# A product of values and weights on VectorE whose inner dimension becomes the head

## The reference

```python
key_e = k[src] + e
alpha = jnp.sum(q[dst] * key_e, axis=-1) / jnp.sqrt(jnp.asarray(C, x.dtype))
m = jax.ops.segment_max(alpha, dst, num_segments=N)
p = jnp.exp(alpha - m[dst])
denom = jax.ops.segment_sum(p, dst, num_segments=N)
w = p / (denom[dst] + 1e-16)
msg = (v[src] + e) * w[..., None]
agg = jax.ops.segment_sum(msg.reshape(E, heads * C), dst, num_segments=N).reshape(N, heads, C)
```

## Time and profile before

| | |
|---|---|
| median of 3 runs | 7181.92 us (7181.11 to 7182.72) |
| profiled execution | 7166.77 us, its span 7165.0 us |
| busy over the span | PE 81%, POOL 67%, VectorE (DVE) 64%, ACT 47% |
| multi-head stage | about 2426 to 4846 us of the span |
| messages (L886) | 488 instructions, 332.3 us, 681 ns each |

### The profile page before, as it was taken

How to read it: one execution, slowest core, us unless ns; L and a number is a source line. 1 busy time by engine, 2 the same in 40 slices (tenths; PEclk the granted TensorE clock), 3 DMA queues, 4 the chain that set the end, 5 groups by cost and what they waited for, 6 DMA issues and landing times. The chain is left out here.

```text
span 7165.0 us, 172653 instructions
## 1 busy us (share of the span) xinstructions
PE 5823.4 (81%) x39803; PEld 4591.0 (64%) x39803; DVE 4571.8 (64%) x12911; ACT 3369.3 (47%) x8069; POOL 4776.0 (67%) x4738
## 2 busy tenths in 40 slices
PE   3688888898766577777777877876889999999997
PEld 2667777777764366666677767773555555666666
DVE  4344455555567577888889999995444555555554
ACT  2334444445444345555556666652334444444442
POOL 0677777777772377777777777642777777777760
PEclk7787888899887676777778787777999999999999
DMA  2455565566544666666666666656455555555552
GB/s 79 126 142 146 150 155 156 157 167 170 126 92 112 203 186 185 187 191 192 196 195 199 199 199 197 193 147 172 107 109 112 115 119 119 121 123 122 122 118 62
DMA packets 1111078, 1069.51 MB, mean 149 GB/s; under 512 B 399272, under 2 KB 882780, under 8 KB 1110068
## 3 DMA queue, kind: packets, MB, share of 16 engines
q1 hardware_dynamic: 934900, 646.58, 33.1%
q0 software_dynamic: 175168, 411.90, 23.4%
HBM read 892.39 MB, written 165.49 MB: 148 GB/s over the span
## 5 line engine op out<-in xcount | busy, mean ns | idle before, releaser
L792 POOL DMA_INDIRECT ring_multi<-kv_rows,src_cols x1564 | 1772.1, 1133 | 630.3 <-issue 478.9
L1153 POOL DMA_INDIRECT ring_pool<-pool_rows,src_cols x1564 | 1481.6, 947 | 644.3 <-issue 459.7
L1153 POOL DMA_INDIRECT ring_single<-h_rows,src_cols x1564 | 1480.9, 947 | 563.2 <-issue 463.5
L993 PE MATMUL ps_q_multi<-query_multi,onehotT_multi 128*128 128x128 bf16 x5856 | 537.7, 258 | 562.6 <-DVE prod_multi L905 559.7
L993 PEld LDWEIGHTS ps_q_multi<-query_multi,onehotT_multi 128*128 128x128 bf16 x5856 | 449.9, 117 | 656.4 <-issue 653.3
L1316 ACT ACTIVATE row_single<-ring_single 128x512 f32 x488 | 308.2, 632 | 1150.8 <-POOLq L1144 729.1
L1316 ACT ACTIVATE row_pool<-ring_pool 128x520 f32 x488 | 309.2, 634 | 1127.3 <-POOLq L1144 1110.7
L982 PE MATMUL ps_d_multi<-message_multi,onehot 128*128 128x136 f32 x3904 | 731.2, 346 | 0.0
L871 DVE TENSOR_TENSOR x_rows<-ring_multi,term_multi 128x1024 f32<-128x1024 f32 x488 | 593.6, 1216 | 166.0 <-POOLq L783 150.9
L1233 DVE CUSTOM_DVE_ANT_0 masked_single<-mask_single,ps_s_single,start_single 128x512 f32<-128x512 bf16 x488 | 364.6, 747 | 500.2 <-PE ps_s_single L1264 436.0
L982 PEld LDWEIGHTS ps_d_multi<-message_multi,onehot 128*128 128x128 f32 x3904 | 670.6, 251 | 0.8 <-issue 0.2
(11 more groups left out here) (222 smaller groups left out, 12259.9 us busy)
## 6 DMA issues: line engine op xcount, KB each, us to landing
term_multi<-edge_terms SPq DMA_DIRECT2D x488, 256.0 KB
edge_terms<-edge_term SPq DMA_DIRECT2D x391, 256.0 KB
dst_pool<-in_dst_rows SPq DMA_DIRECT2D x488, 128.0 KB
dst_multi<-in_dst_rows SPq DMA_DIRECT2D x488, 128.0 KB
dst_single<-in_dst_rows SPq DMA_DIRECT2D x488, 128.0 KB
query_multi<-query_parts SPq DMA_DIRECT2D x488, 96.0 KB
cols<-query_cols SPq DMA_DIRECT2D x488, 64.0 KB
ring_pool<-pool_rows,src_cols POOLq DMA_INDIRECT x1564
```

The source lines that it names most:

```text
L792: pool.indirect_dma_start(out=ring[:, u, j, :], out_offset=None, in_=g.kv_rows, in_offset=bass.IndirectOffsetOnAxis(ap=g.src_cols[:, c:c + ...
L993: i = T_.matmul(ps_q[n % 2][:, j], onehotT[:, n % TURNED, j], query[:, n % QB, k], start=(k == 0), stop=(k == 2))
L1153: pool.indirect_dma_start(out=ring[:, u, j, :], out_offset=None, in_=rows, in_offset=bass.IndirectOffsetOnAxis(ap=g.src_cols[:, c:c + 1], ...
```

## The change

L886 computes the same products from the same tiles. Its three access patterns walk the dimensions in another order: the channel outside and the head inside. The output steps by 17 words from one element to the next and the values by 16; the weights step by 17 and are read again for each of the 16 channels. Before, channels were inside: rows of 16 adjacent words on output and values, and one weight repeated 16 times.

```diff
-                    V.tensor_tensor(out=message[:, m, :, :, 0:HEAD_DIM],
-                                    in0=value(weighed).rearrange("p j (h c) -> p j h c", h=H),
-                                    in1=message[:, m, :, :, HEAD_DIM:HW].to_broadcast([P, J, H, HEAD_DIM]), op=ALU.mult)\
+                    V.tensor_tensor(out=message[:, m, :, :, 0:HEAD_DIM].rearrange("p j h c -> p j c h"),
+                                    in0=value(weighed).rearrange("p j (h c) -> p j c h", h=H),
+                                    in1=message[:, m, :, :, HEAD_DIM:HW].rearrange("p j h c -> p j c h")
+                                    .to_broadcast([P, J, HEAD_DIM, H]), op=ALU.mult)\
                      .then_inc(E["message"].sem, 1)
```

## The result

The changed kernel took 7240.09 us (median of 4 runs, 7228.54 to 7264.67) beside 7182.32 before: 1.0085 times the time, 95% interval [1.0062, 1.0107]. A second set of 5 runs of the same kernel, beside its own runs of the kernel before, gave 1.0097 [1.0080, 1.0115], 70 us.

The account below looks back on a forecast made before the run. VectorE was taken to bound late items directly and early ones through gathers held until L886 ends; 149 us late plus 124 us early made 273, added to 7181.92: 7455 us, 8-in-10 range 7310 to 7570.

Parts of the forecast that it names:

- late regime: Output stage from about 3700 us, 257 items: VectorE is the bound, each item pays 0.58 us, 149 us together.
- early regime: First 231 items of the stage: L886 was taken to hold gathers, so 213 items pay 0.58 us, 124 us.
- rival 3: GpSimd's gathers slip in between elements of the slower L886; VectorE's early wait hides most growth; 7346 us, chance 0.07.
- I take half of it, 2.17 ns.: Price of an L886 element with half the possible extra for stepped output: L886 takes 1258 ns, 0.58 us more.
- Rival 1: Only L886's stepped reads cost, its stepped write is free: 1063 ns, 0.38 us more, 7361 us, chance 0.22.
- The three rows for reads: L352, L1643 and L922, existing instructions with stepped reads, gave 1.79, 1.68 and 1.56 ns an element.
- the row for writes: L852, a memset of 64 words 9 apart: 0.84 ns a word against 0.83 for adjacent words, so stepping seemed free.
- Rivals 2 and 4: First: L886 at 3.0 ns or more an element, 7652 us, chance 0.11; second: L886 keeps 681 ns, 7182 us, 0.05.
- the caught gather: Gather starting while L871 runs: expected to take some 2.1 us and still end 0.22 us behind an L886.
- the wait for L783: VectorE's wait for GpSimd's word that a block has landed, at L871: expected to stay near 150 us.

Follow-up runs that it names:

- the moved form: L886 with channels inside, as in the kernel before, moved from before the scan to between L922 and L927; 0.9856 of the kernel before.
- the forms: Eleven forms of a 128x512 instruction run alone on scratch data ahead of the stage's loop; flat 691 ns, all three operands stepped 1038 ns.
- the run with the plain instruction: Kernel before, channels inside, plus a 128x268 product of adjacent words into a spare tile right behind L886; 1.0101, 7261.86 us.

## Why the prediction was wrong

*What bounds the kernel.* The late regime was read rightly: a closed chain of VectorE, every ns of L886 counts. It was 4.56 us and is 4.90.

*"So in the early regime the cycle is: word of the block, L871, L886, end of the caught gather."* This step failed. 365 gathers that end 0.21 to 0.23 us behind an L886 were read as held by it, and so 213 early items were charged with L886's whole growth, 124 us. The gathers end 0.82 us behind L871, and L886 only ran beside their last 0.82 us. The changed profile and the moved form show it. L886 holds only gathers that start in it, 134 in the changed kernel. So the early items hid most of their growth: the first two groups of 61 items grew by 0.11 and 0.03 us and the third shrank by 0.10, where 0.347 was added to L886. That is the size of rival 3, but not its reason: no gather slips in between the elements of the slower L886, for 207 of the 208 that start in it before its last 0.08 us end 0.82 us behind it.

*"I take half of it, 2.17 ns."* This term was mis-sized. The rows gave 1.79 ns an element for stepped reads, and 1.75 was measured in place ((1043 - 147) / 512). The added price for the output was not there: one, two or three stepped streams cost 1012 to 1038 ns. L886 grew by 0.36 and not by 0.58 us. Rival 1 has the number (1063) but its reason, that a stepped output costs nothing, is refuted by L880 of the forms: 1020 ns for the output alone. The three rows for reads (1.79, 1.68 and 1.56) were all good within 0.2 ns an element; the row for writes, a memset of 64 words, was not.

The Trainium skill, "Vector Engine (DVE) Microarchitecture Reference", section 5.2, has 1.71 to 1.76 ns a column for one or both sources or the output hopping, 1.98 for all three. The runs differ from it in the last: here it was 1.69 to 1.70 for one, 1.71 for both inputs and 1.74 for all three ((1038 - 148) / 512). The 2.50 of its small steps didn't appear at 16 and 17 words.

*The rivals.* The sizes of rivals 1 and 3 came in together, and each had been priced alone, at 7361 and 7346. Together, with the late 257 items alone: 257 x 0.36 = 93, 7275. The range left no room for both, though nothing in the one speaks against the other. The measured 58 to 70 us lie 23 to 35 below that. Part of it is that the late items did not pay in full either: groups 5 and 6 were still above VectorE's 4.556 before and grew by 0.22 and 0.32 us. Part is L927, which lost 19 us. How the rest divides between gathers that were held less and the scatter of single executions was not separated. Rivals 2 and 4 did not come.

*What would show it.* The list named the right places to look: late items are 4.90 us and not 5.17, and the caught gather ends inside L886, its sign for rival 3. Of the wait for L783 it said that it would nearly vanish under rival 3; it fell by a third only, from 150.9 to 100.1 us, and the first two groups of items, above the floor of 4.90 us, still go by the gathers.

## What to carry to other kernels

A fixed distance to the end of an instruction is no sign that it released something: test it against the instruction before it, and look for cases where the two differ in length. When two engines alternate as the bound over a stage, cost a change by item: each pays only what lifts it above the other engine's pace. Where a closed chain of an engine has a short wait for its own result, put an independent instruction there: moving L886 into the gap of 0.31 us made this kernel 1.4% faster, though some of that may come from the gathers.

## What was not expected of the hardware

- A stepped float32 access costs 0.32 us on 512 elements, the same for an input or the output, and hardly more for all three (1012 to 1038 ns against 691). Pairs of adjacent words took 725 ns, even with half of the output rows at an odd word.
- A GpSimd gather (0.95 us) that starts while VectorE runs an instruction with both inputs in SBUF ends 0.82 us behind that instruction, in 365 + 32 + 10 cases before and 434 behind L871 in the moved form. With two such instructions 0.25 us apart 171 gathers that started in the first and 51 that started in between ended 0.82 us behind the second. The rule is not complete: in the run with the plain instruction 96 gathers of 1.05 to 1.07 us ended 0.83 us behind the key product, one of whose inputs stands in PSUM.
- It works the other way too: an L927 that starts within 0.05 us of a gather takes 0.228 us, another 0.167.
- Making an item longer at the old place of L886 made its gathers shorter (284, 175 and 73 us above 0.95 for 0, 0.35 and 0.60 us); with 0.60 us more the first groups of items became shorter than before. At the new place it was the other way round (192 and 282 us for 0 and 0.35).
